# Group statistics by lane shuffles, the maxima's rows in one DMA, and the first two score tiles fed through diagonal matrices

## The reference

```python
# per block, per image; g: group norm with 32 groups (2 channels each)
h = group_norm(x)                       # mean and variance over 2 channels x 1024 points
q, k, v = Wq @ h + bq, Wk @ h + bk, Wv @ h + bv        # 64 x 1024 each
scores  = q.T @ k * 64 ** -0.5          # 1024 x 1024
attn    = softmax(scores, axis=-1)
x       = x + Wo @ (attn @ v) + bo
```

## Time and profile before

| | us |
|---|---|
| median of 3 runs | 207.44 |
| lowest and highest | 205.97, 207.63 |
| the profiled execution | 205.8 |
| its span in the trace | 204.0 |

### The profile page before, as it was taken

The page is one execution under the profiler, slowest core; times in us unless marked ns, Lnnn a source line. Parts: engine busy times, 40 slices in busy tenths (PEclk is TensorE's granted clock), DMA queues, the critical chain, the costliest instruction groups (busy, mean ns, idle before and its releaser), DMA issues.

```text
span 204.0 us, 3287 instructions
## 1 busy us (share of the span) xinstructions
PE 193.1 (95%) x1252; PEld 103.7 (51%) x1252; DVE 139.9 (69%) x190; ACT 105.3 (52%) x147; POOL 147.1 (72%) x88
## 2 busy tenths in 40 slices
PE   8889887999999999999999999999999998999980
PEld 8756655555445546455455454554544544554420
DVE  1468955667497768866795769675985559906964
ACT  2467444465575448554746466535954443457500
POOL 1252207779779988999799988998799959998003
PEclk9969996999999999999999999999999999999999
DMA  5224020210004000400040001300041000010101
...
DMA packets 4719, 7.06 MB, mean 35 GB/s; under 512 B 800, under 2 KB 1760, under 8 KB 4704
## 3 DMA queue, kind: packets, MB, share of 16 engines
q1 hardware_dynamic: 4272, 6.33, 12.3%
q10 hardware_dynamic: 432, 0.53, 0.7%
...
## 4 chain that ended last, share of the span: by engine, by line
PE 85%; DVE 11%; issue 2%; POOL 0%; ACT 0%; DVEq 0%; POOLq 0%
PE ps_attn L692 26%; PE ps_max L652 9%; PE ps_scores L672 8%; PE ps_scores L676 6%; PE ps_scores L674 6%; PE ps_scores L680 6%; DVE neg_part L489 5%; PE ps_misc L640 4%; PE ps_scores L632 4%; PE ps_misc L699 3%; PE ps_scores L617 2%; DVE rden L505 2%; PE ps_scores L681 2%; PE ps_misc L713 1%; DVE rden L601 1%
## 5 line engine op out<-in xcount | busy, mean ns | idle before, releaser
L247 POOL TENSOR_TENSOR prob_sum<-prob_sum,probs 128x1024 f32<-128x1024 f32 x43 | 102.7, 2388 | 14.7 <-ACT probs L349 10.4
L489 DVE TENSOR_REDUCE neg_part<-ps_max 128x2 f32<-128x1024 f32 x59 | 71.9, 1218 | 38.1 <-PE ps_max L653 38.0
L349 ACT ACTIVATE probs<-ps_scores 128x1024 f32<-128x1024 f32 x64 | 63.2, 1025 | 48.4 <-PE ps_scores L681 46.2
L692 PE MATMUL ps_attn<-probs,vals 128*64 128x512 f32 x256 | 61.8, 604 | 0.0
L652 PE MATMUL ps_max<-keys,q_hi 64*128 64x512 f32 x59 | 28.1, 477 | 2.0 <-DVE neg_part L489 1.3
L505 DVE RECIPROCAL rden<-den 128x128 f32<-128x128 f32 x28 | 25.1, 926 | 7.0 <-ACT den L355 7.0
L692 PEld LDWEIGHTS ps_attn<-probs,vals 128*64 128x64 f32 x256 | 15.8, 136 | 27.7 <-issue 20.0
L653 PE MATMUL ps_max<-keys,q_hi 64*128 64x512 f32 x59 | 28.1, 476 | 0.0
L672 PE MATMUL ps_scores<-q_hi,keys 64*128 64x512 f32 x64 | 26.5, 414 | 0.0
L673 PE MATMUL ps_scores<-q_hi,keys 64*128 64x512 f32 x64 | 26.5, 414 | 0.0
L680 PE MATMUL ps_scores<-q_row,ones_r 64*128 64x512 f32 x64 | 25.5, 399 | 0.0
...
## 6 DMA issues: line engine op xcount, KB each, us to landing
...
q_row<-max_rows SPq DMA_DIRECT2D x16, 2.0 KB
...
```

What stands on the lines that cost most here:

```text
L247: pool.tensor_tensor(prob_sum[u % 2][:, :], first[:, :], probs[t][:, :], ALU.add).then_inc(added, 1)
L349: act.activation(probs[t][:, :], ps_scores[t % 2][:, :], ACT.Exp, scale=SCALE).then_inc(exp_done, 1)
L489: dve.tensor_reduce(neg_part[u % 2][:, at:at + JS + 1:JS], ps[:, :].rearrange("p (h n) -> p h n", h=2), AX.X, ALU.max, negate=True).then_i ...
L692: mm = pe.matmul(ps_attn[half * C:(half + 1) * C, :], v, probs[t][:, cols], start=(t == 0), stop=(t == TILES - 1))
```

## The change

- Statistics: `gn_own`, `gn_about`, `gn_var` and the four small matmuls of each unit go. A new `gn_group` on VectorE takes a partition's statistics, exchanges them with the neighbour's by a lane shuffle, exchanges the pairs between the upper and the lower 64 partitions by two more shuffles, aggregates all four sets, and writes `var_eps` and `neg_mean`. It runs where `gn_own` ran; `gn_affine(w + 2)` now stands between row maxima 2 and 3.
- The maxima's rows go to `q_row` in one DMA instead of two.
- Unit 0: score tiles 0 and 1 no longer use `q_row`. ScalarE and VectorE scale the identity by the columns of `neg_max[0]` into `max_diag` (two and six blocks of 128 x 128), and TensorE multiplies a 128-row `ones_r` by it. The three product pairs of these two tiles move ahead of the loop.
- The start: the setup of layer 1 moves forward on TensorE and ScalarE; VectorE's row maximum 1 of unit 1 moves behind `gn_group(2)`, TensorE's product 1 of unit 1 to iteration 0; `keep_warm` counts change from 20, 16, 4, 12 to 20, 12, 5. Half of `consts` is loaded.

```diff
@@ -165,7 +166,7 @@
             return 32 * (unit // RING + 1)
 
         def last_row(unit):
-            return 32 * (unit // 2 + 1)
+            return 16 * (unit // 2 + 1)
 
         block = ctx.enter_context(nc.Block())
 
@@ -190,9 +191,8 @@
                 sp.wait_ge(max_staged, u + 1)
                 if u < 2:
                     sp.wait_ge(rows_zero, u + 1)
-                for n in range(2):
-                    row = q_row[u % 2][n * C:n * C + 1, :].bitcast(F32).rearrange("p (t n) -> p t n", t=JS)
-                    sp.dma_start(row, max_rows[n * JS:(n + 1) * JS, :].bitcast(F32)).then_inc(row_in[u % 2], 16)
+                rows = q_row[u % 2][0:P:C, :].bitcast(F32).rearrange("p (t n) -> p t n", t=JS)
+                sp.dma_start(rows, max_rows[:, :].bitcast(F32)).then_inc(row_in[u % 2], 16)
 
             def store(image):
                 unit = UNITS - B + image
@@ -297,7 +297,7 @@
 
         @block.scalar
         def _(act):
-            act.dma_start(const_sb[:, :], consts).then_inc(consts_in, 16)
+            act.dma_start(ident[:, :], consts[:, 0:P]).then_inc(consts_in, 16)
             for n in range(LAYERS):
                 act.dma_start(layer[n][:, :], layer_params[n]).then_inc(params_in[n], 16)
 
@@ -340,6 +340,13 @@
                     act.wait_ge(row_in[(u - 1) % 2], last_row(u - 1))
                 act.wait_ge(max_turned, u + 1)
                 act.activation(max_rows[:, :], ps_misc[0:TILES, 0:P], ACT.Copy).then_inc(max_staged, 1)
+
+            def diagonals():
+                act.wait_ge(consts_in, 16)
+                act.wait_ge(max_ready, 1)
+                for t in range(2):
+                    act.activation(max_diag[:, t * P:(t + 1) * P], ident[:, :], ACT.Copy,
+                                   scale=neg_max[0][:, t:t + 1]).then_inc(diag_act, 1)
 
             def exp(u, t):
                 act.wait_ge(scores_mm, TILES * u + t + 1)
@@ -400,6 +407,7 @@
             affine(1)
             apply_norm(1)
             copy_v(0)
+            setup(1)
             high_q(1)
             high_k(1)
             full(1)
@@ -407,8 +415,8 @@
             bias_x(0)
             bias_x(1)
             spread_biases(1)
+            diagonals()
             stage_max(0)
-            setup(1)
             for w in range(UNITS):
                 prep = w + 2 < UNITS
                 exp(w, 0)
@@ -436,26 +444,22 @@
 
         @block.vector
         def _(dve):
-            def gn_own(u):
+            def gn_group(u):
                 base = GN * u
-                dve.bn_stats(stats6[:, :], xs[:, slot(u)]).then_inc(gn_step, 1)
+                if u:
+                    dve.wait_ge(gn_step, base)
+                    dve.wait_ge(rstd_ready, u)
+                dve.bn_stats(stats[:, 0:STATS], xs[:, slot(u)]).then_inc(gn_step, 1)
                 dve.wait_ge(gn_step, base + 1)
-                dve.bn_aggr(own[:, :], stats6[:, :]).then_inc(gn_step, 1)
-
-            def gn_about(u):
-                base = GN * u
-                dve.wait_ge(mean_mm, u + 1)
-                dve.tensor_scalar(neg_mean[:, :], ps_misc[:, 0:1], -2.0, None, ALU.mult).then_inc(gn_step, 1)
-                dve.tensor_scalar(dev[:, :], ps_misc[:, 0:1], -2.0, own[:, 0:1],
-                                  ALU.mult, ALU.add).then_inc(gn_step, 1)
+                dve.stream_shuffle(stats[:, STATS:2 * STATS], stats[:, 0:STATS], PAIRED).then_inc(gn_step, 1)
+                dve.wait_ge(gn_step, base + 2)
+                dve.stream_shuffle(stats[0:C, 2 * STATS:4 * STATS], stats[C:P, 0:2 * STATS], IN_PLACE)
+                dve.stream_shuffle(stats[C:P, 2 * STATS:4 * STATS], stats[0:C, 0:2 * STATS], IN_PLACE).then_inc(gn_step, 1)
+                dve.wait_ge(gn_step, base + 3)
+                dve.bn_aggr(group[:, :], stats[:, :]).then_inc(gn_step, 1)
                 dve.wait_ge(gn_step, base + 4)
-                dve.tensor_scalar(var_about[:, :], dev[:, :], dev[:, :], own[:, 1:2],
-                                  ALU.mult, ALU.add).then_inc(gn_step, 1)
-
-            def gn_var(u):
-                dve.wait_ge(var_mm, u + 1)
-                dve.tensor_scalar(var_eps[:, :], ps_misc[:, 1:2], 2.0, EPS[u // B],
-                                  ALU.mult, ALU.add).then_inc(var_ready, 1)
+                dve.tensor_scalar(var_eps[:, :], group[:, 1:2], EPS[u // B], None, ALU.add).then_inc(var_ready, 1)
+                dve.tensor_scalar(neg_mean[:, :], group[:, 0:1], -1.0, None, ALU.mult).then_inc(gn_step, 1)
 
             def gn_affine(u):
                 base = GN * u
@@ -524,25 +528,25 @@
                 dve.tensor_tensor(LATE[:, :], first[:, :], probs[t][:, :], ALU.add).then_inc(late_added, 1)
 
             dve.wait_ge(x_in[0], 16)
-            gn_own(0)
-            gn_about(0)
-            gn_var(0)
+            gn_group(0)
             dve.wait_ge(params_in[0], 16)
             gn_affine(0)
             dve.wait_ge(x_in[1], 16)
-            gn_own(1)
-            gn_about(1)
+            gn_group(1)
             dve.wait_ge(biases_set, 1)
             dve.wait_ge(proj_mm, 1)
             dve.tensor_scalar(q_hi[0][:, :], ps_scores[0][:, 0:HALF], bias_q[0][:, :], None,
                               ALU.add).then_inc(q_hi_done, 1)
-            gn_var(1)
             for t in range(TILES):
                 row_max(0, t, (ps_max, ps_scores[1])[t % 2])
-            row_max(1, 0, ps_max)
-            row_max(1, 1, ps_scores[1])
+            dve.wait_ge(consts_in, 16)
+            dve.wait_ge(max_ready, 1)
+            for t in range(2, TILES):
+                dve.tensor_scalar(max_diag[:, t * P:(t + 1) * P], ident[:, :], neg_max[0][:, t:t + 1], None,
+                                  ALU.mult).then_inc(diag_dve, 1)
+            row_max(1, 0)
             dve.wait_ge(x_in[2], 16)
-            gn_own(2)
+            gn_group(2)
             for b in range(3, B):
                 dve.wait_ge(x_in[b], 16)
 
@@ -550,15 +554,14 @@
                 prep = w + 2 < UNITS
                 nxt = w + 1 < UNITS
 
+                if w == 0:
+                    row_max(1, 1)
                 if nxt:
                     row_max(w + 1, 2)
                 if prep:
-                    gn_about(w + 2)
+                    gn_affine(w + 2)
                 if nxt:
                     row_max(w + 1, 3)
-                if prep:
-                    gn_var(w + 2)
-                    gn_affine(w + 2)
                 if nxt:
                     row_max(w + 1, 4)
                 if w and prep:
@@ -589,7 +592,7 @@
                 if w + 3 < UNITS:
                     if w + 3 >= B:
                         dve.wait_ge(final_done, w + 3 - B + 1)
-                    gn_own(w + 3)
+                    gn_group(w + 3)
                 if w == LAST:
                     for t in range(EARLY + 1, TILES - 1):
                         add_late(t)
@@ -616,14 +619,6 @@
                 for _ in range(times):
                     pe.matmul(ps[0:C, 0:C], ones[:, :], ones[:, :], start=True, stop=True)
 
-            def group_mean_of(u):
-                pe.wait_ge(gn_step, GN * u + 2)
-                pe.matmul(ps_misc[:, 0:1], half_group_mean, own[:, 0:1], start=True, stop=True).then_inc(mean_mm, 1)
-
-            def group_var_of(u):
-                pe.wait_ge(gn_step, GN * u + 5)
-                pe.matmul(ps_misc[:, 1:2], half_group_mean, var_about[:, :], start=True, stop=True).then_inc(var_mm, 1)
-
             def project(u):
                 p = layer[u // B]
                 pe.wait_ge(h_ready, u + 1)
@@ -654,10 +649,10 @@
 
             def turn_max(u):
                 pe.wait_ge(max_ready, u + 1)
-                pe.transpose(ps_misc[0:TILES, 0:P], neg_max[u % 2][:, :], ident).then_inc(max_turned, 1)
-
-            def scores(u, t):
-                q, ql, k, row = q_hi[u % RING], q_lo[u % RING], keys[u % RING], q_row[u % 2]
+                pe.transpose(ps_misc[0:TILES, 0:P], neg_max[u % 2][:, :], ident[:, :]).then_inc(max_turned, 1)
+
+            def products(u, t):
+                q, ql, k = q_hi[u % RING], q_lo[u % RING], keys[u % RING]
                 if t == 0:
                     pe.wait_ge(k_lo_swapped[u % RING], last_swap(u))
                     pe.wait_ge(q_lo_done, u + 1)
@@ -675,10 +670,25 @@
                 pe.matmul(right, k[low, b:b + P], ql[low, :], start=False, stop=False)
                 pe.matmul(left, k[top, a + HALF:a + HALF + P], q[top, 0:HALF], start=False, stop=False)
                 pe.matmul(right, k[low, b + HALF:b + HALF + P], q[low, 0:HALF], start=False, stop=False)
-                if t == 0:
+
+            def less_max(u, t):
+                row, ps = q_row[u % 2], ps_scores[t % 2]
+                if t == (0 if u else 2):
                     pe.wait_ge(row_in[u % 2], last_row(u))
-                pe.matmul(left, ones_r[top, :], row[top, :], start=False, stop=True)
-                pe.matmul(right, ones_r[low, :], row[low, :], start=False, stop=True).then_inc(scores_mm, 1)
```

(58 more changed lines are left out.)

17 lines of the change are left out of this document (9 added, 8 removed).

## The result

The kernel after takes 208.16 us (median of 4 runs, 207.06 to 209.16), the kernel before, run beside it, 206.70 (4 runs, 204.15 to 207.63). The ratio is 1.0144, with a 95% interval of 1.009 to 1.0198: slower by 0.9 to 2.0%. It is more than the 0.7% between the two medians, because ratios here compare fast executions alone, and two of the four of the kernel before (207.44 and 207.63) lie over 1.5% above its fastest. The profiled execution took 209.16 with a span of 207.4, against 205.8 and 204.0 before.

The account below looks back on a forecast made before the run. TensorE's issue was taken to bound the steady part, with GpSimd close behind. Terms -1.4 (iteration 0), -0.45 (iteration 1) and 4 x 0.63 made +0.7 us on 207.44: 208.1, own range 206 to 209.5, wider range 203.4 to 211.5.

Parts of the forecast that it names:

- A: End of GpSimd's sums of tiles 4 to 7 in an iteration; M was forecast no earlier than A + 2.30.
- M: Mark on TensorE: each iteration's fourth maxima product, next_max(4) ahead of scores(w, 2); forecast 22.52 us apart, 21.89 before.
- M of 1 to M of 5: Four steady iterations, each forecast 0.63 us longer because the affine step ahead of row maximum 3 closes a loop.
- rival 1: Steady iterations: the loop doesn't close, each takes 21.27 us, -4.5 in sum, so 202.9; chance 0.17.
- rival 2: Steady iterations: TensorE's wait ahead of M lets the clock fall every time, +4.5 on the forecast, 212.6; chance 0.13.
- the estimate of 2.6: Upper bound in us for VectorE's statistics group, if each shuffle pairs with a mask load; 1.84 was forecast.
- Rival 4: VectorE's shuffles cost 1 us or more each, so row maximum 2 sets M: +2 to +3, 210.6; chance 0.08.
- it begins near 7.9: Start: the first projection, freed of the mean matmul ahead of it, begins near 7.9 us, 1.5 earlier.
- Rival 3: Start: the clock falls around 12 us as before, product 3 comes only 0.9 earlier, +1.9, 210.0; chance 0.15.
- I assume the lower clock costs as much behind M as now: Assumption for M of iteration 0 to M of iteration 1, forecast 0.45 us shorter than 23.24.
- Alone this would make an iteration 21.27: Steady iterations: dropping TensorE's statistics matmuls saves 0.62 us of 21.89, by TensorE's work alone.
- slower by over 1%: Outcome class for the whole kernel, over 209.5 us; chance 0.30, against 0.48 for within and 0.22 for faster.

Follow-up runs that it names:

- e4: The kernel before with only gn_var and gn_affine(w + 2) moved ahead of row maximum 3 on VectorE; 208.32 us, ratio 1.0182 to the kernel before.
- e1: The changed kernel with gn_affine(w + 2) moved back behind row maximum 3 on VectorE; 202.25 us, ratio 0.9899 to the kernel before.
- e3: The changed kernel without the diagonals, score tiles 0 and 1 of unit 0 subtracting through q_row; 206.77 us, ratio 1.0072 to the kernel before.
- e7: The changed kernel with the maxima's rows in two DMAs as in the kernel before; 207.53 us, ratio 1.0119 to the kernel before.
- e6: The kernel of e1 with short filler matmuls in TensorE's three gaps of iteration 0; 201.16 us, ratio 0.9805 to the kernel before.
- e11: The kernel of e8 with iteration 0 packed and the statistics' first pass ahead of row maximum 1; 196.89 us, ratio 0.9642 to the kernel before.
- e8: The kernel before with only the new shuffle statistics, affine step behind row maximum 3, no diagonals, old start; 198.72 us, ratio 0.9709.

## Why the prediction was right or wrong

**The affine step ahead of row maximum 3: right, in mechanism and size.** Forecast A + 2.30, measured A + 2.30; TensorE's wait 1.2, measured 1.03; an iteration 22.52, measured 22.5. e4 shows that the move is enough for it, and e1 that without it the rest of the change doesn't close the loop. The term "M of 1 to M of 5" was +2.52 and came out as +2.45. Neither rival 1 nor rival 2 happened: the clock stays at its upper level past 38 us, in spite of the 1.03 us of waiting in each iteration.

**The shuffles: right.** VectorE's time line of after, first group:

```profile
3.89 0.69 DVE L452 BATCH_NORM_STATS2 stats<-xs 128x6 f32<-128x512 f32 x1 [3.89 <-DMA xs<-x_dram]
4.63 0.01 DVE L454 LOAD_MASK_SELECT stats<-stats  x1
4.63 0.16 DVE L454 STREAM_SHUFFLE stats<-stats 128x6 f32<-128x6 f32 x1
4.83 0.01 DVE L456 LOAD_MASK_SELECT stats<-stats  x1
4.86 0.17 DVE L456 STREAM_SHUFFLE stats<-stats 64x12 f32<-64x12 f32 x1
4.95 0.01 DVE L457 LOAD_MASK_SELECT stats<-stats  x1
5.04 0.16 DVE L457 STREAM_SHUFFLE stats<-stats 64x12 f32<-64x12 f32 x1
5.24 0.26 DVE L459 BATCH_NORM_AGGREGATE group<-stats 128x2 f32<-128x24 f32 x1
5.54 0.15 DVE L461 TENSOR_SCALAR var_eps<-group 128x1 f32<-128x1 f32 x1
5.61 0.14 DVE L462 TENSOR_SCALAR neg_mean<-group 128x1 f32<-128x1 f32 x1
```

The three shuffles take 0.16 to 0.17 us each, and the group goes from 3.89 to 5.75, 1.86 us for a forecast 1.84 (its own terms add up to 1.86). The separate mask load of which the Trainium skill tells ("Vector Engine (DVE) Microarchitecture Reference", section 3.8) is there: each shuffle has one in front of it, the third too, whose pattern is that of the second. But the load takes 0.01 us, not a small operation's time, so the estimate of 2.6 that I had hung on that rule doesn't come true. Rival 4 didn't happen either: no shuffle comes near 1 us.

**The diagonals: nearly right.** Six take 1.27 us, forecast 1.45. Each is busy for 0.28 us, inside my bounds of 0.16 and 0.31, and they overlap, so that one starts every 0.20, for the 0.24 that I took. That is near the 0.19 that I had estimated by the perf-mode tier table of "VectorE: DVE Perf Modes" in the Trainium skill; no run here has the same operation from PSUM, so the rate of two to one isn't tested. From the end of row maximum 7 to M of iteration 0 are 9.9 us, forecast 10.0. That `exp(0, 0)` comes early and gains nothing at M is what e3's profile shows.

**The start: the working held in one of two kinds of execution.** Forecast: first projection 7.9, row maximum 3 of unit 0 at 14.45, M at 30.2. e7: 7.86, 14.35, 30.00. The profiled execution of after: 9.09, 16.22, 31.87. What failed is one clause, "it begins near 7.9": I took the end of the fillers for free, and didn't ask at which speed they run. In after's execution the fillers and the first half of the projection run at half speed. Row maximum 3 of unit 0 started at 16.22 there, later than the 15 that I had named as a sign of being wrong. Before's profile shows 32 fillers in 2.08 us, 0.065 apiece, so it had the early start. Rival 3 priced nearly what came, 210.0 for 209.16 in the profiled execution, but by another mechanism: the granted clock doesn't fall at 12 in after, TensorE comes up to full speed late.

**M of iteration 0 to M of iteration 1: wrong.** The step that failed is "I assume the lower clock costs as much behind M as now". Before, 3.4 us behind M were at the lower clock (32.4 to 35.8). After, the clock falls at 27.5, in the gap of 2.38 us ahead of product 2 of unit 1, and comes back at 37.7, 5.8 us behind M. The 2.4 us more at half speed cost half of that, 1.2: -0.45 + 1.2 = +0.75, for +0.68 measured. It shows in A too: before, A came 20.49 behind M of iteration 0 (52.11 - 31.62), after 21.63 (53.50 - 31.87), and M of iteration 1 at A + 2.29, for a forecast A + 2.30. The gaps ahead of M were in my own working ("TensorE is nearly idle from 23 on"); I charged the low clock to the products in them and not to the score tiles after them. e6, which only fills the gaps in e1, takes the loss away.

**The other steps.** The row DMA was put at nothing, and e7 shows no difference. "Alone this would make an iteration 21.27" was 0.11 too low: once the first loop is open, the sums and the denominators hold the iteration at 21.38 (e11, by its waits) and, as it seems, at the 21.40 of e1 and e8. Rival 1's price for a loop that stays open, 202.9, is near e1's 202.25.

**The sum.** 208.1 was forecast and 208.16 measured, which flatters the working. The forecast was a difference of +0.7 us on top of a median of 207.44. In the comparison itself the median of before was 206.70, so that the base of the forecast was 0.74 too high, and the medians differed by 1.46, so that the forecast difference was 0.76 too low. The two errors cancel, and that is luck. Beside the other runs the median of before was 204.68 to 205.16. The ratio gives +1.4%, some 3 us, and e7's +1.2%. In microseconds the time lies in the range and within the limits of 205.4 and 209.5 that I had given 0.48; as a difference it is rather "slower by over 1%", which I had given 0.30, with an interval that begins at 0.9%. Of the 2.7 us between the forecast difference and that of the profiled pair, 1.65 are the start's and 1.1 the clock's behind M. Where the start is the early one (e7), nearly only the latter is left: +1.6 us for +0.7. All of these are against one profile of before, with much low clock; by the ratios after and e7 are 2.4 to 3 us slower.
